# Spreading eight rows of scalars over the partitions: by indicator matmuls, or by DMA

## The chip, the cores and the metric

One core of a Trainium2 chip runs the whole kernel as one program. The metric is the device time in microseconds (us) of one execution. Five engines work side by side: TensorE (PE, matrix products into PSUM), VectorE (DVE), ScalarE (ACT), GpSimd (POOL) and SyncE (SP, which here only issues DMAs). They wait for each other by semaphores. All data is fp32; large products are made of three, from a high and a low part of each operand.

## The reference

```python
x = x + attn(cond(x, side, side, w1, u1, c), Wq, Wk, Wv, Wo, q_scale, k_scale)
x = x + ffn(cond2(x, side, side, w2, u2, c), gate_w, mask_up_w, gate_proj_w, up_proj_w, down_proj_w, inv_map)
```

x is 4 x 256 tokens of 256 channels. cond is a two-sided scan over the tokens, attn a causal attention with 16 heads over 4 key heads, and ffn a feed-forward stage with 8 groups of 176 rows. In ffn each token takes its 8 best of 64 experts. The weights of the chosen experts of one group, added up, give one scalar for each token and group; within a group the experts' shares are a softmax, which weighs a correction that is added to gate and up. Row r of group g then is silu(gate) * up * scalar[g, token], and the down product goes over all 8 x 176 = 1408 rows.

## The kernel before

Channels lie on partitions, tokens along the rows of SBUF. The tokens are worked in two pairs of 512 (PT_). Each engine runs a list of steps, made by `make_plan`: first the scans and the attention of both pairs (32 items), then from about 324 us the feed-forward stage. This stage has 11 tiles of 128 of the 1408 rows (FT = 11) for each pair, 22 tiles in all, numbered f; f = 11 is the first of the second pair. FFN_ORDERS says in which order an engine takes its steps of tile f:

- PE: GA and GB (gate and up of tile f: six products each of 128x512, and one with the expert table EX, two in tile 5 of a pair), GS (line 1289), Y (the down product of tile f-2, six products), and a routing step of the second pair while there are any.
- ACT: GT (tanh, line 792), a routing step, the cast that splits the weights of tile f+3 into high and low part (line 637), GH (the cast of the result to its high part OH, line 800).
- POOL: the low part of the weights of tile f+3 (line 567, three chunks), GL (the low part OL of the result, line 593).
- DVE: GU, three operations: with gate (1078), with up (1082), with the scalars (1087).

The scalars take this way. In step ("route", p, 4) DVE adds the weights of each group into g8a (954) and copies them into STS at columns 0 to 7 and 32 to 39 (956, 957), the rest of which POOL cleared. In ("route", p, 8) PE turns STS (1246) into proj, ACT casts it to SCX (784), and DVE makes the low part in partitions 32 to 39 (980). IND is an indicator: rows g and 32+g are 1 at the columns of group g. It is loaded in two blocks ("ind"), through the three stage buffers that all weights share, and cast by ACT (725). The product GS of a tile of IND with SCX then gives in PSUM (ov) the scalar of each row's group for all 512 tokens. GS waits until the DVE has used the tile before (a_ready), as there is one ov.

SP issues loads in the order of PE's plan; the load into a stage buffer waits for the split of the block that was in it (split_lo, counted by POOL). Weights of tile f+4 therefore load once those of f+1 are split.

Of the kernel before, what the change touches and what calls it, by code (L numbers as in the profile page):

```python
# [6 lines left out]
ALU = mybir.AluOpType  # L7
# [19 lines left out]
NSTAGE, NSLOT, NPS = 3, 6, 4  # L27
# [5 lines left out]
def table_col(g):  # L33
# [24 lines left out]
    "PE": ["GA", "GB", "GS", "Y", "last", "split"],  # L58
# [18 lines left out]
def kv_k(p, half):  # L77
# [17 lines left out]
    "PE": {"R": None, "split": None, "small": None, "ind": None, "K1": None, "V": None, "K3": None, "GA": None, "GB": None,  # L95
           "GS": None, "route": (0, 1, 3, 4, 6, 7, 8)},
    "ACT": {"split": None, "small": None, "ind": None, "K1": None, "V": None, "K2": None, "K3": None, "table": None,
            "wkv": (1, 6, 7), "gate": (0, 1), "route": (0, 2, 3, 5, 6, 7, 8)},
    "DVE": {"K1": None, "K2": None, "table": None, "onehot": None, "wkv": (0, 2, 3, 4, 5, 6, 8), "gate": (0, 1),
            "route": (1, 2, 4, 5, 6, 7, 8)},  # L100
# [14 lines left out]
def make_plan(engine, order, ffn_order):  # L115
# [8 lines left out]
    for i, st in ((2, ("split", "V", 0)), (0, ("R", 6)), (0, ("R", 7)), (0, ("table", 0)), (2, ("table", 1)),  # L124
                  (1, ("onehot",)), (16, ("zeros",)), (24, ("ind", 0)), (32, ("ind", 1)),
                  (11, ("split", "K", 1)), (18, ("split", "V", 1))):
        put(bg, i, st)
# [25 lines left out]
    for f, places in enumerate(([36, 37, 38], [45, 45, 45])):  # L153
        for kind, i in zip(("GA", "GB", "GS"), places):
            if i < END:
                put(bg, i, (kind, f))
                ahead.append((kind, f))
# [61 lines left out]
BLOCKS = [s for s in PLAN if s[0] in ("small", "split", "ind") or s[0] == "R" and s[1] >= 6]  # L219
# [3 lines left out]
BLOCK_COLS = {"R": 4 * FI, "small": 256, "ind": FT * P // 2, "K": 1024, "V": 1024, "Q": 1024, "O": 1024, "F": 768}  # L223
# [84 lines left out]

def program(nc, ins, out):
    ctx = ExitStack()  # L310
    with ctx:
# [31 lines left out]
        IND = sb("IND", [P, FT * P], F32R)  # L343
# [28 lines left out]
        SCX = sb("SCX", [P, B * T], F32R)  # L372
# [22 lines left out]
        STS = sb("STS", [P, TPP, P])  # L395
# [17 lines left out]
        pads_ready decay_ready init_act init_dve zeros_ready key_scale_ready bmask_ready onehot_ready indicator_ready  # L413
# [24 lines left out]
        def wait_proj_free(eng, step):  # L438

            n = PROJ[step]  # L440
            if n == 0:
                return
            q = PROJ_STEPS[n - 1]
            if q[0] in ("K1", "A"):
                eng.wait_ge(s["square_ready"], TOK[q] + 1)
            elif q[0] == "V":
                eng.wait_ge(s["v_ready"], VNO[q] + 1)
            elif q[2] in (0, 3):
                eng.wait_ge(s["rt_act"], RT_ACT[q[2]] + 7 * q[1])
            else:  # L450
                eng.wait_ge(s["rt_vec"], RT_VEC[q[2]] + 7 * q[1])
# [3 lines left out]
        RT_VEC = {1: 1, 2: 2, 4: 3, 5: 4, 6: 5, 7: 6, 8: 7}  # L455
# [84 lines left out]
        def _(pool):  # L540
# [13 lines left out]
            for st in PLANS["POOL"]:  # L554
# [19 lines left out]
                elif st[0] == "zeros":  # L574
                    pool.memset(STS[:], 0.0).then_inc(s["zeros_ready"], 1)
# [22 lines left out]
        def _(act):  # L598
# [13 lines left out]
            for st in PLANS["ACT"]:  # L612
# [109 lines left out]
                elif st[0] == "ind":  # L722
                    w, blk = FT * P // 2, BLOCK_NO[st]
                    act.wait_ge(staged[blk % NSTAGE], 16 * (blk // NSTAGE + 1))
                    nc.scalar.copy(IND[:, w * st[1]:w * st[1] + w], stage[:, blk % NSTAGE, 0:w]).then_inc(s["indicator_ready"], 1)
# [40 lines left out]
                elif st[0] == "route":  # L766
# [16 lines left out]
                    if k == 8:  # L783
                        nc.scalar.copy(SCX[:, tok], proj[:]).then_inc(s["rt_act"], 1)
# [19 lines left out]
        def _(dve):  # L804
# [112 lines left out]
            def route(p, k):  # L917
# [33 lines left out]
                elif k == 4:  # L951
                    dve.wait_ge(s["proj_full"], PROJ[("route", p, 4)] + 1)
                    linked(v.tensor_copy(FL, pj))
                    linked(v.tensor_reduce(g8a[:], FL.rearrange("p a (g j) -> p a g j", g=G), X, ALU.add))
                    dve.wait_ge(s["zeros_ready"], 2)
                    linked(v.tensor_copy(STS[:, :, 0:G], g8a[:]))
                    linked(v.tensor_copy(STS[:, :, 32:32 + G], g8a[:]))
# [20 lines left out]
                elif k == 8:  # L978
                    dve.wait_ge(s["rt_act"], 7 * p + 7)
                    last(v.tensor_tensor(SCX[32:64, tok], proj[32:64, :], SCX[32:64, tok].bitcast(F32), ALU.subtract))  # L980

            for st in PLANS["DVE"]:
# [90 lines left out]
                elif st[0] == "GU":  # L1073
# [9 lines left out]
                    dve.wait_ge(s["scal_full"], f + 1)  # L1083
# [3 lines left out]
                    v.scalar_tensor_tensor(out=PR[:, 4 + f % 2, :], in0=PR[:, 2 + f % 2, :], scalar=0.5, in1=ov[:],  # L1087
# [12 lines left out]
        def _(pe):  # L1100
# [30 lines left out]
            for st in PLAN:  # L1131
# [85 lines left out]
                elif st[0] == "route":  # L1217
# [13 lines left out]
                    elif k == 3:  # L1231
                        pe.wait_ge(s["rt_vec"], 7 * p + RT_VEC[2])
# [7 lines left out]
                    elif k in (6, 7):  # L1240
                        pe.wait_ge(s["rt_vec"], 7 * p + RT_VEC[5])
                        for t in range(TPP):
                            i = tp(proj[:, P * t:P * t + P], ST[:, t, k - 6, :, :, :].rearrange("p g d e -> p (g d e)"), ident)
                    elif k == 8:
                        for t in range(TPP):
                            i = tp(proj[:, P * t:P * t + P], STS[:, t, :], ident)
                    i.then_inc(s["proj_full"], 1)
                elif st[0] in ("GA", "GB"):
# [25 lines left out]
                    pe.wait_ge(s["rt_vec"], 7 * p + 6)  # L1274
# [86 lines left out]
```

## Time and profile before

| | us |
|---|---|
| median of 3 runs (442.9, 447.45, 446.42) | 446.42 |
| profiled execution, its own time | 446.21 |
| its span, first to last instruction | 444.2 |

| engine | busy, us | share |
|---|---|---|
| PE | 380.3 | 86% |
| PE, loading weights | 305.6 | 69% |
| DVE | 336.3 | 76% |
| ACT | 290.4 | 65% |
| POOL | 214.8 | 48% |

Matrix products overlap on PE, so the length of one is more than the time from its start to the next one's. A share is a mean over stages with different limits; what a change in one stage does is read from the rows of that stage. All times of rows are from the start of the span.

### The profile page before, as it was taken

To read this page: it belongs to the slowest core of one execution; us is meant where nothing else is said; L and a number is where in the kernel's file an instruction comes from. 1 tells how busy PE (TensorE), PEld (TensorE's weight loads), DVE (VectorE), ACT (ScalarE), POOL (GpSimd) and SP (SyncE) were. 2 spreads that over 40 slices of the span, in tenths; PEclk is the share of its full clock that TensorE was granted. 3 is DMA by queue.
4 is the path that set the end of the run, shared out by engine and by line. 5 is a ranking of instruction groups with operands and counts; after the bars stand their busy time and mean duration, and the time that the engine had idled before them with its cause. 6 is when DMAs were issued, how large, how long until landed. Compare 5 with 4: busy or idle time off the path is not lost.

```text
span 444.2 us, 6572 instructions
## 1 busy us (share of the span) xinstructions
PE 380.3 (86%) x1974; PEld 305.6 (69%) x1974; DVE 336.3 (76%) x834; ACT 290.4 (65%) x675; POOL 214.8 (48%) x236
## 2 busy tenths in 40 slices
PE   0097866799998869997889798899899999999996
PEld 0086644587877557875758686777678887888884
DVE  6999577999998997577999979866657758553443
ACT  5444868699889768886789995979366334444321
POOL 4671520637553735513159121237138865687632
PEclk9998999999999997999999899999999999999999
DMA  7813410102111110110102200012112321233101
GB/s 201 312 32 106 137 43 0 49 1 97 47 49 48 49 47 0 49 49 0 47 2 82 80 0 2 0 38 71 38 53 90 106 53 56 72 108 94 61 0 47
DMA packets 11073, 26.84 MB, mean 60 GB/s; under 512 B 1312, under 2 KB 3872, under 8 KB 11040
## 3 DMA queue, kind: packets, MB, share of 16 engines
q1 hardware_dynamic: 11040, 26.44, 18.6%
q8 instruction: 16, 0.26, 0.2%
q14 instruction: 17, 0.14, 0.1%
HBM read 25.39 MB, written 1.05 MB: 60 GB/s over the span
## 4 chain that ended last, share of the span: by engine, by line
PE 49%; DVE 30%; ACT 12%; issue 6%; POOL 1%; DMA 1%; POOLq 0%; SPq 0%; DVEq 0%; ACTq 0%
PE acc L1105 4%; PE ov L1198 4%; PE acc L1106 4%; PE acc L1107 4%; PE tr L1127 4%; PE sc L1176 3%; DVE B L845 3%; DVE PR L1037 3%; DVE F L845 3%; ACT PR L600 3%; PE proj L1105 3%; PE proj L1107 2%; PE proj L1106 2%; DVE SS L902 2%; PE tr L1105 2%
## 5 line engine op out<-in xcount | busy, mean ns | idle before, releaser
L567 POOL TENSOR_TENSOR WL<-stage,WH 128x256 fp32r<-128x256 f32 x146 | 119.8, 851 | 112.7 <-ACT WH L637 112.6
L587 POOL TENSOR_TENSOR PR<-PR,RI 128x512 f32<-128x512 f32 x48 | 54.0, 1140 | 89.1 <-DVE RI L1051 89.1
L1105 PE MATMUL proj<-WH,RH 128*128 128x512 f32 x96 | 43.5, 453 | 39.3 <-DVE RL L896 22.9
L600 ACT ACTIVATE PR<-PR,NBI,RQ 128x128 f32<-128x128 f32 (+1 forms) x128 | 68.5, 546 | 1.9 <-DVE NBI L1042 1.7
L1105 PE MATMUL acc<-OH,WH 128*128 128x256 f32 (+1 forms) x172 | 55.4, 322 | 5.2 <-DVE OL L1063 4.4
L1107 PE MATMUL acc<-OH,WL 128*128 128x256 f32 (+1 forms) x172 | 54.0, 314 | 0.0
L1106 PE MATMUL acc<-OL,WH 128*128 128x256 f32 (+1 forms) x172 | 54.0, 314 | 0.0
L1176 PEld LDWEIGHTS sc<-kT,QT 128*128 128x128 f32 x256 | 40.8, 191 | 18.9 <-issue 14.1
L1105 PEld LDWEIGHTS proj<-WH,RH 128*128 128x128 f32 x96 | 19.0, 198 | 47.1 <-issue 42.5
L1176 PE MATMUL sc<-kT,QT 128*128 128x128 f32 (+1 forms) x256 | 47.5, 328 | 2.9 <-DVE MX L1037 2.9
L1198 PE MATMUL ov<-PTS,V 128*128 128x512 f32 x96 | 47.0, 598 | 1.4 <-DVE OL L1063 1.4
L637 ACT CAST WH<-stage 128x768 fp32r<-128x768 f32 (+1 forms) x42 | 39.4, 938 | 2.2 <-DMA stage<-in_wk 2.2
L1078 DVE SCALAR_TENSOR_TENSOR PR<-PR,sc 128x512 f32<-128x512 f32 x22 | 15.1, 685 | 32.2 <-ACT PR L792 32.2
L1107 PE MATMUL proj<-WH,RL 128*128 128x512 f32 x96 | 39.4, 410 | 0.0
L1106 PE MATMUL proj<-WL,RH 128*128 128x512 f32 x96 | 39.1, 408 | 0.0
L1037 DVE CUSTOM_DVE_ANT_0 PR<-sc,const 128x128 f32<-128x128 f32 (+1 forms) x128 | 39.0, 351 | 0.1
L1105 PEld LDWEIGHTS acc<-OH,WH 128*128 128x128 f32 x172 | 33.4, 194 | 7.9 <-issue 5.0
L593 POOL TENSOR_TENSOR OL<-PR,OH 128x512 fp32r<-128x512 f32 x22 | 28.7, 1307 | 12.6 <-ACT OH L800 12.6
L902 DVE TENSOR_REDUCE SS<-SQ 128x4 f32<-128x512 f32 x40 | 27.0, 677 | 10.3 <-ACT SQ L692 10.2
L1106 PEld LDWEIGHTS acc<-OL,WH 128*128 128x128 f32 x172 | 33.5, 195 | 1.7
L1107 PEld LDWEIGHTS acc<-OH,WL 128*128 128x128 f32 x172 | 33.4, 194 | 1.7
L800 ACT CAST OH<-PR 128x512 fp32r<-128x512 f32 x22 | 13.7, 622 | 30.3 <-PE acc L1107 28.4
(167 smaller groups left out, 913.1 us busy)
## 6 DMA issues: line engine op xcount, KB each, us to landing
stage<-in_ffn SPq DMA_DIRECT2D x22, 384.0 KB, 3.1
stage<-in_wq SPq DMA_DIRECT2D x8, 512.0 KB, 3.5
stage<-in_wo SPq DMA_DIRECT2D x8, 512.0 KB, 3.5
PR<-in_tables SPq DMA_DIRECT2D x4, 352.0 KB, 7.1
fT<-in_fT SPq DMA_DIRECT2D x4, 256.0 KB, 4.2
xT<-in_xT SPq DMA_DIRECT2D x4, 256.0 KB, 4.1
stage<-in_wk SPq DMA_DIRECT2D x2, 512.0 KB, 4.6
stage<-in_wv SPq DMA_DIRECT2D x2, 512.0 KB, 3.6
```

The lines of the kernel that those rows point to most:

```text
L567: i = pool.tensor_tensor(lo[:, c:c + 256], src[:, c:c + 256], hi[:, c:c + 256].bitcast(F32), ALU.subtract)
L587: pool.tensor_tensor(pr, pr, RI[:, m % 4, hs[0]:hs[0] + nh].rearrange("p (h o) -> p h o", o=1).broadcast_to([P, nh, 512 // nh]), ALU.mult) ...
L593: pool.tensor_tensor(OL[:, sl], PR[:, 4 + f % 2, :], OH[:, sl].bitcast(F32), ALU.subtract).then_inc(s["a_lo"], 1)
L600: return nc.scalar.activation(o, i, ACT.Exp, **k)
L637: nc.scalar.copy(WH[:, slot, 0:w], src[:, 0:w]).then_inc(s["split_hi"], 1)
L902: v.tensor_reduce(SS[:, n % NST, half_, :], SQ[:, e % 2, :].rearrange("p (h n) -> p h n", h=REP), X, ALU.add).then_inc(s["sumsq_done"], 1)
L1037: i = v.tensor_tensor_reduce(PR[:, u % 6, w * k:w * k + w], sc[u % 2][:, w * k:w * k + w], mask[:, 256 - w:256], 1.0, NEG_BIG, ALU.add, AL ...
L1105: mm(o, lh, rh, start=first, stop=False, skip_group_check=True)
L1106: mm(o, lh, rl, start=False, stop=False, skip_group_check=True)
L1107: return mm(o, ll, rh, start=False, stop=last, skip_group_check=True)
L1176: i = mm(sc[u % 2][:, w * k:w * k + w], QT[:, m % 3, h, :], kT[:, g, T * bb:T * bb + w], start=True, stop=True)
L1198: i = mm(ov[:], V[:, 2 * bb + c, g * D:(g + 1) * D], PTS[:, m % 2, c, :, :].rearrange("p h n -> p (h n)"), start=(c == 0), stop=(c == ti))
```

## The change

The indicator, its loads and casts, the product GS and the low part of the scalars go. DVE adds the groups into SG8, PE turns it into 8 rows, and ACT copies these to SCR, 8 partitions of 1024 tokens, in plain fp32. SP then issues DMAs that read one row of 512 tokens of SCR (2 KB in one partition) and write it into each partition of the tile that belongs to that group. A tile of 128 rows has one or two groups, so one or two DMAs: 18 for a pair, 36 in all. The target is SBC with three buffers (NBC), and the third operation of DVE reads it there, in place of PSUM.

```diff
-NSTAGE, NSLOT, NPS = 3, 6, 4
+NSTAGE, NSLOT, NPS, NBC = 3, 6, 4, 3
-    "PE": ["GA", "GB", "GS", "Y", "last", "split"],
+    "PE": ["GA", "GB", "Y", "last", "split"],
...
+def group_rows(m):
+
+    first, last = P * m // FI, (P * m + P - 1) // FI
+    return [(g, max(g * FI - P * m, 0), min((g + 1) * FI - P * m, P)) for g in range(first, last + 1)]
...
+            def spread_scalars(f):
+                p, m = divmod(f, FT)
+                sp.wait_ge(s["rt_act"], 7 * p + 7)
+                if f >= NBC:
+                    sp.wait_ge(s["a_ready"], f - NBC + 1)
+                for g, lo, hi in group_rows(m):
+                    sp.dma_start(SBC[lo:hi, f % NBC, :], SCR[g:g + 1, p * PT_:(p + 1) * PT_].rearrange("g (o n) -> g o n", o=1).broadcast_to([1, hi - lo, PT_])).then_inc(spread_in[f % NBC], 16)
+
             for n in range(6, len(BLOCKS)):
+                if BLOCKS[n][0:2] == ("split", "F") and BLOCKS[n][2] >= 4:
+                    spread_scalars(BLOCKS[n][2] - 4)
                 load(n)
+            for f in range(FT * NPAIR - 4, FT * NPAIR):
+                spread_scalars(f)
...
-                        nc.scalar.copy(SCX[:, tok], proj[:]).then_inc(s["rt_act"], 1)
+                        nc.scalar.copy(SCR[:, tok], proj[0:G, :]).then_inc(s["rt_act"], 1)
...
-                    linked(v.tensor_reduce(g8a[:], FL.rearrange("p a (g j) -> p a g j", g=G), X, ALU.add))
-                    dve.wait_ge(s["zeros_ready"], 2)
-                    linked(v.tensor_copy(STS[:, :, 0:G], g8a[:]))
-                    linked(v.tensor_copy(STS[:, :, 32:32 + G], g8a[:]))
+                    linked(v.tensor_reduce(SG8[:], FL.rearrange("p a (g j) -> p a g j", g=G), X, ALU.add))
+                    dve.wait_ge(s["zeros_ready"], 1)
...
-                elif k == 8:
-                    dve.wait_ge(s["rt_act"], 7 * p + 7)
-                    last(v.tensor_tensor(SCX[32:64, tok], proj[32:64, :], SCX[32:64, tok].bitcast(F32), ALU.subtract))
...
-                    dve.wait_ge(s["scal_full"], f + 1)
+                    dve.wait_ge(spread_in[f % NBC], 16 * spread_count(f))
...
-                    v.scalar_tensor_tensor(out=PR[:, 4 + f % 2, :], in0=PR[:, 2 + f % 2, :], scalar=0.5, in1=ov[:],
+                    v.scalar_tensor_tensor(out=PR[:, 4 + f % 2, :], in0=PR[:, 2 + f % 2, :], scalar=0.5, in1=SBC[:, f % NBC, :],
...
-                            i = tp(proj[:, P * t:P * t + P], STS[:, t, :], ident)
+                            i = tp(proj[0:G, P * t:P * t + P], SG8[:, t, :], ident)
...
-                elif st[0] == "GS":
-                    f = st[1]
-                    p, m = divmod(f, FT)
-                    if f:
-                        pe.wait_ge(s["a_ready"], f)
-                    else:
-                        pe.wait_ge(s["o_lo"], 32)
-                        pe.wait_ge(s["indicator_ready"], 2)
-                    pe.wait_ge(s["rt_vec"], 7 * p + 7)
-                    mm(ov[:], IND[:, P * m:P * m + P], SCX[:, p * PT_:(p + 1) * PT_], start=True, stop=True).then_inc(s["scal_full"], 1)
```

On SP before, the loads of the 22 tiles of weights (in_ffn) follow the last loads of the output weights and of the indicator, and behind them stand only the stores of the result:

```order
L494 DMA stage<-in_wo 128x1024 x2
L494 DMA stage<-in_ind 128x704
L494 DMA stage<-in_ffn 128x768 x22
L535 DMA out<-xT 128x512 x4
L311 UNCONDITIONAL_BRANCH
```

On SP now, at the same place, with the waits in brackets (rt_act counts ACT's routing copies, a_ready the tiles that DVE has finished):

```order
L502 DMA stage<-in_wo 128x1024 [waits split_lo] x3
L502 DMA stage<-in_ffn 128x768 [waits split_lo] x4
L543 DMA SBC<-SCR 128x1x512 [waits rt_act]
L502 DMA stage<-in_ffn 128x768 [waits split_lo]
L543 DMA SBC<-SCR 48x1x512 [waits rt_act]
L543 DMA SBC<-SCR 80x1x512
L502 DMA stage<-in_ffn 128x768 [waits split_lo]
L543 DMA SBC<-SCR 96x1x512 [waits rt_act]
L543 DMA SBC<-SCR 32x1x512
L502 DMA stage<-in_ffn 128x768 [waits split_lo]
L543 DMA SBC<-SCR 128x1x512 [waits a_ready,rt_act]
```

The first four loads stay together; from then on the spread of tile f stands ahead of the load of tile f+4, up to f = 17, and the spreads of the last four tiles follow the last load. From tile 3 on a spread also waits until DVE has finished tile f-3.

On PE before, between the last product of "up" and the down product of an earlier tile, in the feed-forward stage:

```order
L1278 MATMUL tr<-SX,EX 128x512
L1289 MATMUL ov<-SCX,IND 128x512
L1105 MATMUL acc<-OH,WH 128x512
L1106 MATMUL acc<-OL,WH 128x512
L1107 MATMUL acc<-OH,WL 128x512
```

On PE now:

```order
L1288 MATMUL tr<-SX,EX 128x512
L1115 MATMUL acc<-OH,WH 128x512
L1116 MATMUL acc<-OL,WH 128x512
L1117 MATMUL acc<-OH,WL 128x512
L1115 MATMUL acc<-OH,WH 128x512
```

The product L1289 is gone and nothing else has moved.

## Rows read from the trace of the kernel before

**Rows 1.** The page: busy us of each engine, share of the span, instructions.
```profile
PE 380.3 (86%) x1974; PEld 305.6 (69%) x1974; DVE 336.3 (76%) x834; ACT 290.4 (65%) x675; POOL 214.8 (48%) x236
```
**Rows 2.** Stretches: length, busy us (instructions) of each engine, granted clock, DMA share, GB/s.
```profile
332.00:362.00 30.00, 30.00 (x137) 24.45 (x135) 20.43 (x41) 15.09 (x24) 21.99 (x24) 1.00 0.27 79
386.00:432.00 46.00, 46.00 (x205) 38.09 (x204) 21.42 (x32) 17.56 (x28) 31.91 (x37) 1.00 0.21 64
```
**Rows 3.** PE's timeline, two tiles: start us, us, engine, line, names, shape.
```profile
425.99 0.39 PE L1289 MATMUL ov<-SCX,IND 128*128 128x512 f32 x1
...
430.75 0.39 PE L1289 MATMUL ov<-SCX,IND 128*128 128x512 f32 x1
```
**Rows 4.** What writes ov: durations in ns, min/median/max, first and last start.
```profile
L1289 PE MATMUL ov<-SCX,IND x22: 389/389/389, 331.8 to 435.5; 128*128 128x512 f32 x22
```
**Rows 5.** Timelines of DVE and PE at the first pair's group sums.
```profile
314.35 0.18 DVE L956 COPY STS<-g8a 128x32 f32<-128x32 f32 x1
...
314.79 0.29 DVE L958 TENSOR_SCALAR RT<-RT 128x256 f32<-128x256 f32 x1
...
317.20 0.35 PE L1105 MATMUL acc<-OH,WH 128*128 128x256 f32 x1 [0.95 <-DVE OL L1063]
```
**Rows 6.** Timeline of ACT: the scalars of the first and of the second pair.
```profile
327.53 0.59 ACT L784 CAST SCX<-proj 128x512 fp32r<-128x512 f32 x1 [1.07 <-PE proj L1246]
...
384.45 0.59 ACT L784 CAST SCX<-proj 128x512 fp32r<-128x512 f32 x1 [2.90 <-PE proj L1246]
```
**Rows 7.** The casts of the indicator.
```profile
L725 ACT CAST IND<-stage x2: 797/798/800, 241.0 to 303.4; 128x704 fp32r<-128x704 f32 x2
```
**Rows 8.** The four stores of the result, 256 KB each, from issue to landing.
```profile
DMA to landing us min/median/max: 2.0/2.8/3.8
```
**Rows 9.** DMA from 440 to 444.2, two stores: GB/s in 40 slices, the queue.
```profile
GB/s 0 0 0 0 0 0 0 0 0 0 0 0 0 0 0 0 0 0 195 429 371 371 371 351 332 332 429 371 371 410 390 234 39 0 0 0 0 0 0 0
...
q1 hardware_dynamic: 288, 0.52, 33.4%
```
**Rows 10.** DMA from 395 to 398.5, one load of 384 KB.
```profile
q1 hardware_dynamic: 144, 0.39, 38.2%
```
**Rows 11.** Timeline of DVE, ACT and POOL at the first tiles of the second pair.
```profile
388.44 0.69 DVE L1087 SCALAR_TENSOR_TENSOR PR<-PR,ov 128x512 f32<-128x512 f32 x1
...
389.30 0.62 ACT L800 CAST OH<-PR 128x512 fp32r<-128x512 f32 x1 [1.79 <-PE acc L1107]
...
390.83 0.60 ACT L792 ACTIVATE PR<-sc 128x512 f32<-128x512 f32 x1 [0.91 <-PE sc L1278]
...
391.33 0.83 ACT L637 CAST WH<-stage 128x768 fp32r<-128x768 f32 x1
391.33 1.31 POOL L593 TENSOR_TENSOR OL<-PR,OH 128x512 fp32r<-128x512 f32 x1
...
392.58 2.17 POOL L567 TENSOR_TENSOR WL<-stage,WH 128x256 fp32r<-128x256 f32 x3
```
**Rows 12.** Timeline of DVE and ACT at the last tile.
```profile
436.49 0.69 DVE L1087 SCALAR_TENSOR_TENSOR PR<-PR,ov 128x512 f32<-128x512 f32 x1
...
437.35 0.62 ACT L800 CAST OH<-PR 128x512 fp32r<-128x512 f32 x1 [2.63 <-PE acc L1107]
...
440.38 1.38 DVE L1096 TENSOR_TENSOR xT<-xT,acc 128x512 f32<-128x512 f32 x2 [3.20 <-PE acc L1107]
```
**Rows 13.** A stretch as in rows 2, and PE's timeline in it.
```profile
164.00:170.00 6.00, 3.65 (x14) 3.02 (x15) 5.79 (x22) 3.34 (x8) 3.17 (x4) 0.64 0.20 79
...
166.34 1.94 PE L1127 MATMUL tr<-const,RT 128*128 128x128 f32 x8 [3.08 <-DVE PTS L1057]
```
**Rows 14.** Timeline of DVE and POOL at the first tiles of the first pair.
```profile
333.18 0.69 DVE L1087 SCALAR_TENSOR_TENSOR PR<-PR,ov 128x512 f32<-128x512 f32 x1
...
333.64 3.13 POOL L567 TENSOR_TENSOR WL<-stage,WH 128x256 fp32r<-128x256 f32 x3 [2.51 <-ACT WH L637]
333.78 1.68 DVE L990 SCALAR_TENSOR_TENSOR TH<-TH,fT 128x1024 f32<-128x1024 f32 x1
```

More of the change, by code:

```diff
@@ L94 @@
 RELEVANT = {
-    "PE": {"R": None, "split": None, "small": None, "ind": None, "K1": None, "V": None, "K3": None, "GA": None, "GB": None,
-           "GS": None, "route": (0, 1, 3, 4, 6, 7, 8)},
-    "ACT": {"split": None, "small": None, "ind": None, "K1": None, "V": None, "K2": None, "K3": None, "table": None,
+    "PE": {"R": None, "split": None, "small": None, "K1": None, "V": None, "K3": None, "GA": None, "GB": None,
+           "route": (0, 1, 3, 4, 6, 7, 8)},
+    "ACT": {"split": None, "small": None, "K1": None, "V": None, "K2": None, "K3": None, "table": None,
             "wkv": (1, 6, 7), "gate": (0, 1), "route": (0, 2, 3, 5, 6, 7, 8)},
     "DVE": {"K1": None, "K2": None, "table": None, "onehot": None, "wkv": (0, 2, 3, 4, 5, 6, 8), "gate": (0, 1),
-            "route": (1, 2, 4, 5, 6, 7, 8)},
+            "route": (1, 2, 4, 5, 6, 7)},
     "POOL": {"split": None, "small": None, "zeros": None},
@@ L124, in make_plan @@
     for i, st in ((2, ("split", "V", 0)), (0, ("R", 6)), (0, ("R", 7)), (0, ("table", 0)), (2, ("table", 1)),
-                  (1, ("onehot",)), (16, ("zeros",)), (24, ("ind", 0)), (32, ("ind", 1)),
+                  (1, ("onehot",)), (16, ("zeros",)),
                   (11, ("split", "K", 1)), (18, ("split", "V", 1))):
@@ L153, in make_plan @@
     for f, places in enumerate(([36, 37, 38], [45, 45, 45])):
-        for kind, i in zip(("GA", "GB", "GS"), places):
+        for kind, i in zip(("GA", "GB"), places):
             if i < END:
@@ L217 @@
 PLAN = PLANS["PE"]
-BLOCKS = [s for s in PLAN if s[0] in ("small", "split", "ind") or s[0] == "R" and s[1] >= 6]
+BLOCKS = [s for s in PLAN if s[0] in ("small", "split") or s[0] == "R" and s[1] >= 6]
 BLOCK_NO = {s: n for n, s in enumerate(BLOCKS)}
@@ L222 @@
 SPLIT_NO = {s: n for n, s in enumerate(SPLITS)}
-BLOCK_COLS = {"R": 4 * FI, "small": 256, "ind": FT * P // 2, "K": 1024, "V": 1024, "Q": 1024, "O": 1024, "F": 768}
+BLOCK_COLS = {"R": 4 * FI, "small": 256, "K": 1024, "V": 1024, "Q": 1024, "O": 1024, "F": 768}
 PROJ_SPLITS = [s for s in SPLITS if s[0] == "split" and s[1] in "KVQ"]
@@ L306, with spread_count @@
         unit_tr[units_before(_m) + _j] = TR[("D", _m, _j)]
+def group_rows(m):
+    first, last = P * m // FI, (P * m + P - 1) // FI
+    return [(g, max(g * FI - P * m, 0), min((g + 1) * FI - P * m, P)) for g in range(first, last + 1)]
+def spread_count(f):
+    return sum(len(group_rows(k % FT)) for k in range(f % NBC, f + 1, NBC))
 def program(nc, ins, out):
@@ L342, in program @@
         GWL = sb("GWL", [P, CH, 128], F32R)
-        IND = sb("IND", [P, FT * P], F32R)
         RH = sb("RH", [P, NPAIR, CH, PT_], F32R)
@@ L371, in program @@
         SX = sb("SX", [P, 2, B * T], F32R)
-        SCX = sb("SCX", [P, B * T], F32R)
+        SCR = sb("SCR", [G, B * T])
+        SBC = sb("SBC", [P, NBC, PT_])
         bmask = V[:, :, :].rearrange("p t n -> p (t n)").rearrange("p (c g d e) -> p c g d e", c=CH, g=G, d=16)
@@ L394, in program @@
         ST = sb("ST", [P, TPP, 2, 4, 4, GS])
-        STS = sb("STS", [P, TPP, P])
+        SG8 = sb("SG8", [P, TPP, G])
         def gate1(b):
@@ L412, in program @@
         names = """consts_in vecs_in cond_in side_in0 side_in1 side_in2 side_in3 x_in0 x_in1 x_in2 x_in3 table_in0 table_in1 table_in2 table_in3 table_in4 table_in5 mup_in imap_in stores_done
-        pads_ready decay_ready init_act init_dve zeros_ready key_scale_ready bmask_ready onehot_ready indicator_ready
+        pads_ready decay_ready init_act init_dve zeros_ready key_scale_ready bmask_ready onehot_ready
         split_hi split_lo ffn_used
@@ L417, in program @@
         scores_full max_ready bias_ready exp_done rinv_ready p_ready pt_act pt_dve ov_full o_hi o_lo wo_done x1_ready
-        gate_full up_full scal_full first_rows tanh_done gate_used up_used a_ready a_hi a_lo y_full result_ready
+        gate_full up_full first_rows tanh_done gate_used up_used a_ready a_hi a_lo y_full result_ready
         den_log rt_act rt_vec dve_link act_link pool_link""".split()
@@ L421, in program @@
         staged = [sem(f"staged{k}") for k in range(NSTAGE)]
+        spread_in = [sem(f"spread_in{k}") for k in range(NBC)]
         block = ctx.enter_context(nc.Block())
@@ L447, in wait_proj_free @@
                 eng.wait_ge(s["v_ready"], VNO[q] + 1)
-            elif q[2] in (0, 3):
+            elif q[2] in (0, 3, 8):
                 eng.wait_ge(s["rt_act"], RT_ACT[q[2]] + 7 * q[1])
             else:
-                eng.wait_ge(s["rt_vec"], RT_VEC[q[2]] + 7 * q[1])
+                eng.wait_ge(s["rt_vec"], RT_VEC[q[2]] + 6 * q[1])
         RT_ACT = {0: 1, 2: 2, 3: 3, 5: 4, 6: 5, 7: 6, 8: 7}
-        RT_VEC = {1: 1, 2: 2, 4: 3, 5: 4, 6: 5, 7: 6, 8: 7}
+        RT_VEC = {1: 1, 2: 2, 4: 3, 5: 4, 6: 5, 7: 6}
         def wait_turned(eng, t):
@@ L574, in _ @@
                 elif st[0] == "zeros":
-                    pool.memset(STS[:], 0.0).then_inc(s["zeros_ready"], 1)
                     pool.wait_ge(s["wkv_dve"], last_call(1, B - 1))
@@ L721, in _ @@
                     i.then_inc(s["table_hi"], 1)
[L722 to L725, printed above, removed]
                 elif st[0] == "B":
@@ L775, in _ @@
                     if k == 2:
-                        act.wait_ge(s["rt_vec"], 7 * p + RT_VEC[1])
+                        act.wait_ge(s["rt_vec"], 6 * p + RT_VEC[1])
                         exp(LG, LG).then_inc(s["rt_act"], 1)
                     if k == 5:
-                        act.wait_ge(s["rt_vec"], 7 * p + RT_VEC[4])
+                        act.wait_ge(s["rt_vec"], 6 * p + RT_VEC[4])
                         exp(MR, MR).then_inc(s["rt_act"], 1)
@@ L1231, in _ @@
                     elif k == 3:
-                        pe.wait_ge(s["rt_vec"], 7 * p + RT_VEC[2])
+                        pe.wait_ge(s["rt_vec"], 6 * p + RT_VEC[2])
                         for t in range(TPP):
@@ L1240, in _ @@
                     elif k in (6, 7):
-                        pe.wait_ge(s["rt_vec"], 7 * p + RT_VEC[5])
+                        pe.wait_ge(s["rt_vec"], 6 * p + RT_VEC[5])
                         for t in range(TPP):
@@ L1273, in _ @@
                         three(bank[:], w[0], w[1], RH[:, p, ch, :], RL[:, p, ch, :], ch == 0, False)
-                    pe.wait_ge(s["rt_vec"], 7 * p + 6)
+                    pe.wait_ge(s["rt_vec"], 6 * p + 6)
                     if f == 0:
@@ L1329 @@
                                  np.where(np.arange(P) % 32 // GS == 1, -1.0, 0.0).astype(f32)[:, None]], axis=1)
-    ind = np.zeros((P, FT * P), f32)
-    for g in range(G):
-        ind[g, g * FI:(g + 1) * FI] = 1.0
-        ind[32 + g, g * FI:(g + 1) * FI] = 1.0
-    a["ind"] = ind
     a["imap"] = np.ascontiguousarray(np.broadcast_to(i["L0_ffn_inv_map"].reshape(1, E), (E, E))).astype(np.int32)
```

4 lines of the change are left out of this document (removed).

## The prediction

> **What bounds the kernel now.** The page comes first: TensorE (PE) is busy for 86% of the span, more than any other engine [rows 1]. The table of stretches then shows where that holds. In the feed-forward stage PE has no idle time at all: 30.00 of 30.00 us from 332 to 362 and 46.00 of 46.00 from 386 to 432, at full granted clock, while VectorE (DVE), ScalarE (ACT) and GpSimd (POOL) are idle for a quarter of it or more [rows 2]. PE's timeline gives the beat: the indicator product of one tile starts at 425.99 and that of the next at 430.75, so a tile takes 4.76 us, 21 products 0.227 us apart (one is issued every 0.227, though each lasts 389 ns, since they overlap) [rows 3]. So before the change the stage runs at PE's beat and everything else has slack.
>
> **What is removed.** 22 indicator products, one per tile, of 389 ns each [rows 4], worth 0.227 us each at PE's beat: 22 x 0.227 = 5.0 us of PE. The tile drops from 4.76 to 4.53 us if PE still sets the beat. In each pair's routing, DVE loses two copies into STS (314.35 to 314.79, 0.44 us, ahead of the OL subtraction for which PE sits idle for 0.95 us in the first pair) [rows 5], and after the last transposes the subtraction of SCX, that stands behind ACT's cast of SCX [rows 6]. ACT loses two casts of IND of 0.80 us [rows 7], POOL a memset, SP two loads; none of them stands in front of an idle PE, so I count them as nothing, and they cannot cost anything.
>
> **What is added.** 22 spreads. Each reads one row (512 fp32, 2 KB) of SCR and writes it into up to 128 partitions: 128 packets of 2 KB, 256 KB in all, sent as one or two DMAs. The bytes written are those of one store of the output. But the source is special: all 128 packets read the same partition (a split tile reads two, neighbours). In a store, sixteen queues each read their own eight partitions. No row of this trace shows many queues reading one partition, so I bound it.
>
> From below, a spread lands like a store of 256 KB: 2.0 to 3.8 us, 2.8 in the median [rows 8]. From above, the row behaves like what one queue alone moves, packet after packet: in the window that holds the last two stores the queues worked 33.4% of 16 x 4.2 us = 22.4 us for 256 packets of data, 0.088 us each, so 128 packets one at a time take 11.2 us. The fullest slices of that window show 429 GB/s, 26.8 per queue: at that rate 256 KB through a single reader takes 9.8 us [rows 9]. Between ends so far apart (2.8 and 11.2) I take 9.8: the reading side is one partition, and what the trace shows that one partition, or the eight of a queue, ever gives at once is one queue's flow. With sixteen queues asking there is always a next packet, hence the rate of the fullest slice and not that of the mean.
>
> The Trainium skill prices just this (SBUF — State Buffer, Door 1: The DMA port swizzle): partitions share 16 ports, partitions 0 to 3 lie on one, and 27.6 GB/s was measured through it, 27.2 as its limit. By that page a spread is an estimated 262144 B / 27.2 GB/s = 9.6 us, and the total below would be 564; no run here shows it yet.
>
> **Why it is then on the path.** 9.8 us is more than twice the 4.53 us of a tile. NBC = 3 buffers keep up to three spreads in the queue, so the fixed latency hides, but the flow does not: DVE's last product of tile f waits for spread f, and OH, OL and the down product follow it. The order also puts load F(f+4) behind spread f on the same SP queue. A load of 384 KB occupies the queues for 38.2% of 16 x 3.5 = 21.4 us, 1.34 each [rows 10]. Queues that end their share of the spread early can start on it, so between 0 and 1.34 us is added per load; I take 0.7. A wait that could add more: spread f+1 is issued only after load F(f+4), which waits until tile f+1's weights are split on POOL, and that split now stands behind tile f-3's OL. From landing f-3 it takes 0.69 (DVE) + 0.62 (OH) + 0.60 (tanh) + 0.83 (cast) + about 3.5 (OL and the three chunks) = 6.2 us [rows 11], while spreads f-2 to f are queued, over 20 us of work. So it never starves. PE's 20 products (4.5 us) lie inside each 10 us.
>
> **The sum.**
> - First spread issued when ACT has copied the scalars: 327.53 + 0.59 = 328.1 [rows 6], less 0.4 for the STS copies: 327.7.
> - It lands after the fixed part of a store (2.0 least landing, less the 0.7 that the packets take: 22.4/16/2 per store [rows 8, 9]) 1.3, and 9.8: 338.8.
> - 21 more spreads: 21 x 9.8 = 205.8. 18 loads (F4 to F21) between them: 18 x 0.7 = 12.6. Last landing at 557.2. The second pair's first spread waits for its own scalars, ready some 3 us after spread 9 lands, when spread 10 is still moving: no gap.
> - Tail: from the last scaling on DVE at 436.49 to the end of the span at 444.2 it is now 7.7 us, OH, OL, six products, the addition and the store [rows 12]. That stays: 564.9.
> - PE idles for half of each tile. From 164 to 170, where it had stood idle for 3.08 us, the granted clock is 0.64 of full, a mixture of both levels [rows 13]. At 1.2 GHz the last six products take 1.3 us more: 566.2. Elsewhere PE at 1.2 GHz (9 us per tile) still fits into 10.
> - The profiled execution took 446.2 us beside a span of 444.2: 2.0 around it. 568.2. It lies at the median of the runs (446.42), so nothing is corrected.
>
> The 5.0 us taken from PE are worth nothing here, since PE no longer sets the beat. Upper end: 11.2 per spread (22 x 1.4 = 30.8) and 1.34 per load (+11.5): 611. Lower end: loads free (-12.6) and no loss of clock (-1.3): 554.
>
> **Rivals.** *Hidden* (the other side). If a spread lands like a store, in 2.8 us, it is there at 330.5, ahead of the first scaling at 333.18 [rows 14]; for tile 11 the scalars are ready at 385.04 [rows 6] and it lands at 387.8 against 388.44 [rows 11]. At 3.8 us it is 0.4 late there; OH of that tile waits for PE until 389.30 anyway, and PE needs the tile two tiles later. Then PE keeps the beat: 21 x 0.227 = 4.8, 0.1 at the last tile (DVE ends at 437.18, and OH waits until 437.35 for PE [rows 12]), 0.6 for the STS copies in two pairs: 440.7 us. It decides as long as spread and load together fit in 4.53 us. A second thing touches this rival: the scaling now reads both inputs from SBUF. Where DVE does that today (L990), three POOL chunks take 3.13 us instead of 2.17 [rows 11, 14]. At most 0.69 us per tile is 3 x 0.74 + 1.30 + 0.69 = 4.2 us of POOL, still under 4.53: nothing.
>
> The Trainium skill also has a rule that speaks for this rival (SBUF — State Buffer, Summary: rules for kernel authors): between SBUF and SBUF reckon with 436 GB/s. That would be an estimated 0.6 us of moving, and the change would be worth its 5 us. I hold it to be meant for transfers over all partitions, as the stores here are (up to 429 in a slice).
>
> *Two packets at a time* from a partition: 4.9 us, 5.6 with a load, still over 4.53. 327.7 + 1.3 + 22 x 4.9 + 12.6 + 7.7 + 2.0 = 459 us.
>
> *Slower than one queue*: if one partition gives half of a queue's rate, 19.6 us per spread, 568 + 22 x 9.8 = 784 us; for 640 it takes 13.1. What speaks for it is only that a queue's flow in the trace comes from eight partitions in turn.
>
> **Chances.** One queue's rate (554 to 611): 0.66. Slower than that: 0.09. Two or more packets at a time, but not hidden: 0.09. Hidden: 0.16. The prediction is 568 us. For 8 in 10 the range must take in the two-packet case and the near part of the slow one: 455 to 640; the likeliest case alone has 554 to 611. About 1% is what a measurement of this kernel tells from no change. The hidden case gains 1.3%, of which a small loss leaves less than 1%: it gives 0.10 to faster and 0.05 to same; the rest of it and of the two-packet case that may come out within 1% adds 0.01. Slower has 0.84.
>
> **What would show it.** Right: the landing time of SBC<-SCR at 10 us and more (more where several are queued), DVE's scaling line with some 100 us of idle time ended by DMA, the DMA share over 0.9 through the feed-forward stage at only about 30 to 40 GB/s, PE at half, tiles some 10.5 us apart for the first 18 and 9.8 for the last four, the stage before 327 unmoved. Wrong: landings of about 3 us and a PE without idle time at 4.53 us per tile (hidden), a beat near 5.6 (two packets), tiles over 12 us apart (slower than a queue), or a beat that is long while the queues stand empty: then it is the waits of SP and not the reading.

## The result and the profile after

The changed kernel takes 550.75 us (median of 4 runs, 550.19 to 553.22), the kernel before 445.08 us (median of 4, 442.9 to 447.45). The ratio is 1.238, interval 1.230 to 1.247: slower by almost a quarter. The profiled execution took 550.44 us with a span of 548.7.

In what follows a spread is the one or two DMAs that bring a tile its scalars. It lands when its semaphore shows that all of it has arrived. The scaling is DVE's third operation of a tile, which reads the spread, and the beat is the distance from the start of one tile's scaling to that of the next.

Stretches of the changed kernel, columns as in [rows 2]:

```profile
332.00:362.00 30.00, 19.28 (x74) 14.64 (x73) 8.47 (x11) 7.18 (x12) 11.62 (x14) 0.77 0.92 67
386.00:432.00 46.00, 30.73 (x122) 23.76 (x122) 17.91 (x29) 11.39 (x19) 17.24 (x21) 0.83 0.91 63
...
521.50:539.50 18.00, 5.86 (x12) 3.66 (x12) 4.14 (x6) 2.23 (x4) 2.54 (x2) 0.67 0.88 46
```

PE, without a gap before, is busy for two thirds of the time in the first two stretches and for a third in the last, and part of that at the lower level of its clock (mean granted clock 0.67 to 0.83 of full). No engine is near its limit. What is full is the second column from the right: the DMA queues are busy for 88 to 92% of the time (27 and 21% before) and move no more than 46 to 67 GB/s (79 and 64 before).

What the queues did from 430 to 480, and the three sizes of DMA with the longest part in it (40 slices of GB/s; KB each, median us from issue to landing):

```profile
GB/s 26 26 116 282 31 26 26 26 26 61 223 107 28 26 28 28 26 80 216 103 28 28 28 26 26 102 212 79 26 26 28 26 29 132 196 62 26 29 26 26
...
q1 hardware_dynamic: 1510, 3.32, 92.1%
...
stage<-in_ffn SPq DMA_DIRECT2D x5, 384.0 KB, 14.1
SBC<-SCR SPq DMA_DIRECT2D x2, 256.0 KB, 15.7
```

The first row points at the cause. While only a spread moves, all sixteen queues together make 26 to 28 GB/s in most slices; in [rows 9] sixteen queues made 429 in the fullest slices, 26.8 each, so this is what one of them made there. In between stand the loads of weights, whose fullest slices show 196 to 282 GB/s.

Who waited, us in total, times, longest:

```profile
ACT OH L815 <- DVE PR L1097: 154.7, 22, 8.7
DVE PR L1097 <- DMA SBC<-SCR: 131.6, 22, 7.2
POOL OL L612 <- ACT OH L815: 124.6, 22, 8.5
PEld acc L1115 <- POOL OL L612: 49.8, 12, 7.6
```

The scaling on DVE waits for the spread in each of the 22 tiles, for 131.6 us in all; ACT's cast waits for the scaling, POOL for the cast and PE for POOL. The starts of the scaling give the beat:

```profile
338.75 0.69 DVE L1097 SCALAR_TENSOR_TENSOR PR<-PR,SBC 128x512 f32<-128x512 f32 x1 [7.17 <-DMA SBC<-SCR]
348.55 0.69 DVE L1097 SCALAR_TENSOR_TENSOR PR<-PR,SBC 128x512 f32<-128x512 f32 x1 [6.45 <-DMA SBC<-SCR]
358.41 0.69 DVE L1097 SCALAR_TENSOR_TENSOR PR<-PR,SBC 128x512 f32<-128x512 f32 x1 [6.51 <-DMA SBC<-SCR]
...
378.01 0.69 DVE L1097 SCALAR_TENSOR_TENSOR PR<-PR,SBC 128x512 f32<-128x512 f32 x1 [6.50 <-DMA SBC<-SCR]
387.20 0.69 DVE L1097 SCALAR_TENSOR_TENSOR PR<-PR,SBC 128x512 f32<-128x512 f32 x1 [4.11 <-DMA SBC<-SCR]
...
521.58 0.69 DVE L1097 SCALAR_TENSOR_TENSOR PR<-PR,SBC 128x512 f32<-128x512 f32 x1 [6.44 <-DMA SBC<-SCR]
531.35 0.69 DVE L1097 SCALAR_TENSOR_TENSOR PR<-PR,SBC 128x512 f32<-128x512 f32 x1 [6.42 <-DMA SBC<-SCR]
539.52 0.69 DVE L1097 SCALAR_TENSOR_TENSOR PR<-PR,SBC 128x512 f32<-128x512 f32 x1 [4.82 <-DMA SBC<-SCR]
```

9.8 us per tile at the start, with loads between the spreads, and 9.77 near the end (521.58 to 531.35), with none. 256 KB in 9.8 us is 26.7 GB/s. Before, the beat was 4.76 us [rows 3].

### The profile page after: what moved, and what is told of

The parts are those of the page before. It is cut to its first block, busy times and chain, and to the rows that moved or that the text cites. A ratio compares the mean times of both kernels' runs of the same rounds, so it can differ in the third digit from the quotient of the medians.

```text
span 548.7 us, 6550 instructions
## 1 busy us (share of the span) xinstructions
PE 396.1 (72%) x1952; PEld 309.8 (56%) x1952; DVE 333.1 (61%) x828; ACT 287.2 (52%) x673; POOL 213.5 (39%) x235
## 4 chain that ended last, share of the span: by engine, by line
DVE 23%; PE 22%; SPq 17%; DMA 14%; ACT 13%; issue 7%; POOL 2%; POOLq 0%; ACTq 0%; DVEq 0%
DMA SBC<-SCR 14%; SPq L543 12%; SPq L502 5%; PE ov L1208 3%; ACT PR L619 3%; PE tr L1137 3%; DVE B L860 2%; PE sc L1186 2%; PE proj L1115 2%; DVE PR L1047 2%; DVE F L860 2%; PE acc L1115 2%; PE proj L1117 2%; PE proj L1116 2%; PE acc L1116 2%
## 5 line engine op out<-in xcount | busy, mean ns | idle before, releaser
L587 POOL TENSOR_TENSOR WL<-stage,WH 128x256 fp32r<-128x256 f32 x146 | 117.4, 834 | 105.6 <-ACT WH L656 105.5
L1115 PE MATMUL acc<-OH,WH 128*128 128x256 f32 (+1 forms) x172 | 60.6, 352 | 60.0 <-POOL OL L612 44.4
L1097 DVE SCALAR_TENSOR_TENSOR PR<-PR,SBC 128x512 f32<-128x512 f32 x22 | 15.2, 692 | 131.6 <-DMA SBC<-SCR 131.6
L1115 PEld LDWEIGHTS acc<-OH,WH 128*128 128x128 f32 x172 | 34.7, 202 | 68.1 <-POOL OL L612 49.8
L1116 PE MATMUL acc<-OL,WH 128*128 128x256 f32 (+1 forms) x172 | 57.7, 335 | 0.0
L1117 PE MATMUL acc<-OH,WL 128*128 128x256 f32 (+1 forms) x172 | 57.7, 335 | 0.0
L1117 PEld LDWEIGHTS acc<-OH,WL 128*128 128x128 f32 x172 | 35.2, 205 | 2.8
L1116 PEld LDWEIGHTS acc<-OL,WH 128*128 128x128 f32 x172 | 35.2, 205 | 1.7
L917 DVE TENSOR_REDUCE SS<-SQ 128x4 f32<-128x512 f32 x40 | 27.0, 677 | 11.1 <-ACT SQ L711 10.9
## 6 DMA issues: line engine op xcount, KB each, us to landing
stage<-in_ffn SPq DMA_DIRECT2D x22, 384.0 KB, 14.1
```

What stands on the lines that cost most here:

```text
L587: i = pool.tensor_tensor(lo[:, c:c + 256], src[:, c:c + 256], hi[:, c:c + 256].bitcast(F32), ALU.subtract)
L1115: mm(o, lh, rh, start=first, stop=False, skip_group_check=True)
L1116: mm(o, lh, rl, start=False, stop=False, skip_group_check=True)
L1117: return mm(o, ll, rh, start=False, stop=last, skip_group_check=True)
```

## The experiments

**Another source.** The spread reads row for row from an SCR widened to 128 partitions. PE and ACT fill it from a scratch tensor, so this kernel leaves out the scalars of the groups; the DMAs differ in their source alone:

```diff
-sp.dma_start(SBC[lo:hi, f % NBC, :], SCR[g:g + 1, p * PT_:(p + 1) * PT_].rearrange("g (o n) -> g o n", o=1).broadcast_to([1, hi - lo, PT_])).then_inc(spread_in[f % NBC], 16)
+sp.dma_start(SBC[lo:hi, f % NBC, :], SCR[lo:hi, p * PT_:(p + 1) * PT_]).then_inc(spread_in[f % NBC], 16)
```

> The changed kernel with one thing other: each spread reads row for row from 128 partitions of a wider SCR, no longer one partition for all. Same number of DMAs, same bytes, same order, same waits (the values of the scalars are wrong: this leaves out the choice of the group's row). Theory A (one partition gives about 26.8 GB/s to all readers together): spreads land in 2 to 4 us, DVE's scaling never waits for DMA, PE keeps a beat of 4.53 us per tile, total 440 to 443 us. Rival B (36 more DMAs and their waits on SP hold up the loads): stays at about 550 us, long issue times on SP. Rival C (DMA between SBUF and SBUF is slow by itself): stays at about 550 us.

Measured: 440.69 us against 444.29 of the kernel before, run beside it, ratio 0.994 (0.991 to 0.997). The same 36 DMAs of the same bytes in the same order now land so (us, least, median, longest):

```profile
DMA to landing us min/median/max: 1.9/3.2/5.0
```

For the changed kernel this row reads:

```profile
DMA to landing us min/median/max: 12.1/14.9/22.6
```

(These are from the issue, at which the spread ahead is still moving; so it is more than 9.8.) DVE never waited for a spread, and PE was busy for 46.00 of 46.00 us from 386 to 432. So neither the number of DMAs, nor their order on SP, nor DMA between SBUF and SBUF as such makes the change slow (rivals B and C). The source does: one partition, read by all.

**Half the row.** The spread copies 256 of the 512 tokens, 1 KB packets, and DVE reads the half twice. The kernel leaves out the scalars of the other half.

```diff
-SCR[g:g + 1, p * PT_:(p + 1) * PT_].rearrange("g (o n) -> g o n", o=1).broadcast_to([1, hi - lo, PT_])
+SCR[g:g + 1, p * PT_:p * PT_ + PT_ // 2].rearrange("g (o n) -> g o n", o=1).broadcast_to([1, hi - lo, PT_ // 2])
```

> The changed kernel with spreads of 256 of the 512 tokens (1 KB packets, same 36 DMAs, same single source partition); DVE reads the half twice, so the second half of each pair's tokens gets wrong scalars. Theory A: 4.9 us per spread, against a PE beat of 4.53: 326.6 + 1.3 + 22 x 4.9 + 7.7 to 9.2 + 1.7 = 445 to 447 us, the beat set by DMA by a hair. Rival B (count and order of DMAs): about 550 us still. Rival D (a fixed price per packet at one partition, whatever its size): 9.8 us per spread still, about 550 us.

Measured: 450.21 us, ratio 1.016 (1.011 to 1.021). In the second pair the scaling mostly starts every 5.0 us and still waits for DMA:

```profile
396.23 0.69 DVE L1097 SCALAR_TENSOR_TENSOR PR<-PR,SBC 128x512 f32<-128x512 f32 x1 [1.60 <-DMA SBC<-SCR]
...
401.24 0.69 DVE L1097 SCALAR_TENSOR_TENSOR PR<-PR,SBC 128x512 f32<-128x512 f32 x1 [1.65 <-DMA SBC<-SCR]
```

Half the bytes, half the beat: it is a flow and no price per packet (rival D). It came out 3 us above the forecast: in the middle of the first pair PE, which has the second pair's routing to do there, is slower than 5 us per tile, and the spreads have to start anew for the second pair (the first scaling there waits 3.89 us). This fits the prediction's condition, that a spread costs time once it takes longer than PE's 4.53 us: at 5.0 us it costs 1.6% of the kernel's time, at 9.8 us 24%. No run lies closer to 4.53.

**Partition or port?** After its last store the kernel before issues more DMAs, each waited for, with nothing else running (the waits between them are left out here):

```diff
+sp.dma_start(dst[:, 0:512], src[0:1, 0:512].rearrange("g (o n) -> g o n", o=1).broadcast_to([1, P, 512])).then_inc(s["probe"], 16)   # L538
+sp.dma_start(dst[:, 0:512], src[:, 0:512]).then_inc(s["probe"], 16)             # L540
+sp.dma_start(dst[:, 0:512], ins["wk"][0:1, 0:512].broadcast_to([P, 512])).then_inc(s["probe"], 16)   # L542
+sp.dma_start(dst[0:16:4, :], src[0:4, :]).then_inc(s["probe"], 16)              # L544, 4 rows of 12 KB
+sp.dma_start(dst[0:16:4, :], src[0:16:4, :]).then_inc(s["probe"], 16)           # L546
+sp.dma_start(dst[0:4, :], src[0:16:4, :]).then_inc(s["probe"], 16)              # L548
+sp.dma_start(dst[:, 0:512], src[0:1, 0:512].rearrange("g (o n) -> g o n", o=1).broadcast_to([1, P, 512])).then_inc(s["probe"], 16)   # L550
+sp.dma_start(dst[:, 512:1024], src[4:5, 0:512].rearrange("g (o n) -> g o n", o=1).broadcast_to([1, P, 512])).then_inc(s["probe2"], 16)   # L551, not waiting for L550
```

> The kernel before, and after its last store eight DMAs one after the other, each waited for (the last two together), nothing else running. Expected landings by theory A as it stands (the limit is a port shared by several partitions): one partition to 128, 256 KB: 1.3 + 9.8 = 11 us; 128 to 128 partitions, 256 KB: 2.0; one HBM row to 128: 2 to 3; partitions 0 to 3 to partitions 0, 4, 8, 12, 48 KB: 1.3 + 1.8 = 3.1; partitions 0, 4, 8, 12 to the same: 1.3 + 0.45 = 1.8; partitions 0, 4, 8, 12 to 0 to 3: 3.1 if writing is limited like reading; two spreads at once from partitions 0 and 4: the second lands at 11 to 12 us after its issue if they lie on two ports and the queues overlap, at 21 if not. Rival E (the limit is the single partition, not a port): partitions 0 to 3 land in 1.8 us like 0, 4, 8, 12.

SP's timeline. Each DMA is issued when the one ahead has landed, so the distance of two starts is the landing time of the first (that of L538 starts at 438.0):

```profile
449.26 0.54 SPq L540 DMA_DIRECT2D PR<-stage  x1
451.66 0.35 SPq L542 DMA_DIRECT2D PR<-in_wk  x1
454.73 0.74 SPq L544 DMA_DIRECT2D PR<-stage  x1
458.36 0.63 SPq L546 DMA_DIRECT2D PR<-stage  x1
460.66 0.58 SPq L548 DMA_DIRECT2D PR<-stage  x1
464.05 0.53 SPq L550 DMA_DIRECT2D PR<-stage  x1
465.02 0.53 SPq L551 DMA_DIRECT2D PR<-stage  x1
```

| DMA | expected | landed after, us |
|---|---|---|
| one partition to 128, 256 KB | 11 | 11.3 |
| 128 to 128 partitions, 256 KB | 2.0 | 2.4 |
| one HBM row to 128, 256 KB | 2 to 3 | 3.1 |
| partitions 0 to 3 to 0, 4, 8, 12, 48 KB | 3.1 | 3.6 |
| partitions 0, 4, 8, 12 to the same | 1.8 | 2.3 |
| partitions 0, 4, 8, 12 to 0 to 3 | 3.1 | 3.4 |

Each of these DMAs ran once, in one execution. Four neighbouring partitions take 1.3 us longer to read than four partitions that lie four apart. 48 KB at 26.8 GB/s are 1.8 us and at four times that 0.5, a difference of 1.4. Nor did the neighbours' packets go one after the other: each DMA is four packets of 12 KB (and four small ones), and in the 3.63 us of the one (L544) they took 11.5% of sixteen queues' time, 1.7 us each, about as long as all four together need at that rate; in the other (L546) it was 7.3% of 2.30 us, 0.7 us each. So the limit is not the single partition (rival E), but something that partitions 0 to 3 share and 0, 4, 8, 12 do not. Writing to 0 to 3 also took 1.1 us longer, but there the packets took only 0.5 us each, so what holds it up is not seen in them. The two spreads at once took until 17.8 us after the second was issued, 18.8 for both: two in a row at 9.8 are 19.6 and the fixed part. So two sources that don't share the limit overlap little. That each queue works through the first spread before it comes to the second would explain it; no run tests this. The trace of the changed kernel has the same little gain: where a tile takes its rows from group 3 and group 4, and so reads partition 3 and partition 4, its scaling follows after 9.2 us in the first pair (378.01 to 387.20 above) and 8.6 in the second, not 9.8.

**By way of HBM.** Each pair's eight rows are stored to HBM first (16 KB) and the spreads read them there, the whole result being computed:

```diff
+if m == 0:
+    sp.dma_start(bounce[:, p * PT_:(p + 1) * PT_], SCR[:, p * PT_:(p + 1) * PT_]).then_inc(s["bounced"], 16)
+    sp.wait_ge(s["bounced"], 16 * p + 16)
...
-    sp.dma_start(SBC[lo:hi, f % NBC, :], SCR[g:g + 1, ...]...
+    sp.dma_start(SBC[lo:hi, f % NBC, :], bounce[g:g + 1, p * PT_:(p + 1) * PT_].broadcast_to([hi - lo, PT_])).then_inc(spread_in[f % NBC], 16)
```

> The changed kernel, but each pair's 8 rows are first stored to HBM (16 KB, SP waits for the landing), and the spreads read them there; result complete. Theory A: the single partition is no longer read, so spreads land in about 3 us; the store adds some 2 us ahead of tiles 0 and 11, where 2 to 3 us are spare; 441 to 444 us, below the kernel before. Rival C: HBM reads are as quick as those of loads, same result. If 128 reads of one HBM row are as serial as those of one partition, about 550 us.

Measured: 442.34 us against 444.29, ratio 0.996 (0.992 to 0.999); once more, beside dram_psum below, 443.05 against 444.8, 0.997 (0.994 to 0.999).

> via_dram once more, on the same chip as dram_psum, for the comparison of the two: 0.996 of the kernel before, as measured.

128 reads of one row of HBM are as quick as a spread from 128 partitions: landings of 1.9 to 5.8 us, 3.4 in the median (1.9, 5.0 and 3.2 in wide_source). Only the first spread of each pair is late, by 0.76 and 1.89 us, and the second lateness reaches no idle PE (46.00 of 46.00 us busy from 386 to 432).

**Two buffers.** NBC = 2 in the changed kernel.

> The changed kernel with NBC = 2: a spread is issued once DVE has finished the tile two before, not three. Theory A (flow of the one reader): at that moment one spread of 9.8 us is still moving, the next is issued 1 us after the landing, so nothing changes, 549 to 552 us. Rival F (the waits of SP for a free buffer set the beat, three buffers being just too few): one less buffer adds about the fixed part of a landing, 1.3 to 2 us per tile, 30 us and more in all, 580 us or above.

Measured, in one execution: 551.12 us, the beat unchanged (first scaling at 339.3, last at 540.2, in place of 338.7 and 539.5). The waits for a free buffer don't set the beat (rival F falls).

**One SBUF input in place of two.** wide_source and via_dram gained less than the 5.5 us that the prediction gave the hidden case. In wide_source the scaling, which now reads PR and SBC, both in SBUF, took 0.69 us at times and much more at others. Its durations in ns, least, median, longest:

```profile
L1098 DVE SCALAR_TENSOR_TENSOR PR<-PR,SBC x22: 692/1080/1611, 332.9 to 432.8; 128x512 f32<-128x512 f32 x22
```

and the longest one beside POOL, in their timelines:

```profile
341.56 1.61 DVE L1098 SCALAR_TENSOR_TENSOR PR<-PR,SBC 128x512 f32<-128x512 f32 x1
```

```profile
341.33 1.29 POOL L613 TENSOR_TENSOR OL<-PR,OH 128x512 fp32r<-128x512 f32 x1
343.29 2.13 POOL L588 TENSOR_TENSOR WL<-stage,WH 128x256 fp32r<-128x256 f32 x3 [0.68 <-ACT WH L657]
```

POOL's operation ends at 342.62 and the scaling, started early in it, at 343.17, 0.55 us later: it has waited for POOL. The Trainium skill says so (SBUF — State Buffer, Who interferes with whom): a DVE operation with two SBUF inputs and a GpSimd one that reads SBUF exclude each other, whichever comes second waits until the first is done. The trace agrees: 1.61 us here, and 0.69 us in every tile before, with ov in PSUM. To test what it costs, the second operation writes to the PSUM bank that the indicator product has left free (in tile 0 it first waits until the attention has done with that bank):

```diff
-v.tensor_tensor(PR[:, 2 + f % 2, :], PR[:, 2 + f % 2, :], tr[f % 2][:], ALU.mult).then_inc(s["up_used"], 1)
+v.tensor_tensor(ov[:], PR[:, 2 + f % 2, :], tr[f % 2][:], ALU.mult).then_inc(s["up_used"], 1)
...
-v.scalar_tensor_tensor(out=PR[:, 4 + f % 2, :], in0=PR[:, 2 + f % 2, :], scalar=0.5, in1=SBC[:, f % NBC, :],
+v.scalar_tensor_tensor(out=PR[:, 4 + f % 2, :], in0=ov[:], scalar=0.5, in1=SBC[:, f % NBC, :],
```

> via_dram with one thing other: DVE's second operation of a tile (with up) writes its result to the PSUM bank ov, which no indicator product uses any more, and the third reads it there beside SBC. So the scaling has one input in SBUF, not two. Theory S (the scaling with two SBUF inputs holds up POOL and is held up by it: 0.69 to 1.61 us in wide_source, three POOL chunks up to 3.6 us, and PE waits 1.4 to 1.6 us for it in the first pair): the scaling takes 0.69 us in every tile, POOL's chunks 2.2 us beside it, and the total is 1 to 1.6 us below via_dram. Rival (the loss in the first pair has another source, the store ahead of the spreads): no difference to via_dram.

Measured: 441.98 us against 444.8, ratio 0.994 (0.992 to 0.997). The scaling:

```profile
L1105 DVE SCALAR_TENSOR_TENSOR PR<-ov,SBC x22: 690/692/693, 329.9 to 428.6; 128x512 f32<-128x512 f32 x22
```

Every one takes 0.69 us. What this is worth is read from PE, by the last product of "up" in tiles 2 and 3; first via_dram2:

```profile
337.28 0.39 PE L1293 MATMUL tr<-SX,EX 128*128 128x512 f32 x1
...
344.56 0.39 PE L1293 MATMUL tr<-SX,EX 128*128 128x512 f32 x1
```

then dram_psum:

```profile
334.58 0.39 PE L1296 MATMUL tr<-SX,EX 128*128 128x512 f32 x1
...
340.49 0.39 PE L1296 MATMUL tr<-SX,EX 128*128 128x512 f32 x1
```

7.28 us has become 5.91, and before the change it was 6.12, with one indicator product (0.227 us) more. From tile 0 to tile 21 the same product is at a distance of 99.17 us in dram_psum, 100.82 in via_dram2 and 103.71 before: 1.65 us less than via_dram2, 1.37 of them from tile 2 to 3. In the total it is 1.1 us below via_dram2. The intervals of the two ratios (0.992 to 0.997 and 0.994 to 0.999) overlap, but run against run dram_psum is the quicker one in 115 of 144 pairs. So the mechanism is shown, and a worth of about 1 us is likely, but its size is not pinned down. (Only one execution of each was traced, and that of dram_psum was the quickest of its twelve, 438.37 us; so only distances within the stage are set side by side.)

## Why the prediction was right

**That it gets slower, and where.** Right. The source of the spreads sets the beat, with PE idle for a third of the time and more, at a reduced clock, and the 5.0 us taken from it without effect. Of the signs it named, 30 to 40 GB/s was too low (63 to 67 in the two long stretches): a spread and a load in a beat of 10.5 us make 62, by its own sizes.

**Price of a spread.** 9.8 us was taken, from the fullest slices of a store [rows 9]; measured 9.8 from scaling to scaling, and 11.3 alone with its fixed part, for which 11.1 had been reckoned. That the fullest slice, and not the mean, gives the limit was a choice, and it held. The first scaling was forecast at 338.8 and came at 338.75, which is luck: the spread was issued at 326.63, 1.1 us ahead of the 327.7 reckoned, and no spread landed in less than 12.1 us, where 11.1 had been reckoned. The prediction also took the single partition, or the eight of a queue, as what is limited; the runs show that partitions 0 to 3 share the limit. For the price of a spread this makes no difference, as a tile reads one row or two. The Trainium skill's 9.6 us would have done as well: by its port limit (SBUF — State Buffer, Door 1: The DMA port swizzle) the total was 564. Here the runs back it in more than the price: by that section partitions 0 to 3 lie on one port, and these four read together took 3.6 us where 0, 4, 8 and 12 took 2.3.

**Price of a load between the spreads.** Wrong: 0.7 us for each of 18, 12.6 in all; measured 0. The beat is 9.8 us with loads (348.55 to 358.41) and 9.77 without (521.58 to 531.35). As the spreads are held by their source and not by the queues, a load finds room: its fullest slices show 196 to 282 GB/s in the middle of it. It was in the range, as the lower end (554), and it makes up most of the distance from 568 to 550.

**21 spreads of 9.8.** 205.8 forecast, 200.8 measured (338.75 to 539.52). The distance from one tile to the next is less than 9.8 in four places: 7.7 at the last tile of the first pair and 8.2 at that of the second (531.35 to 539.52), where no spread stood behind it for most or all of its time, and 9.2 and 8.6 where a tile reads groups 3 and 4. This had no term in the sum: 5.0 us. That a spread behind competes for the source and so delays the one ahead is a reading of these distances, not tested.

**Tail and clock.** 7.7 + 1.3 = 9.0 forecast, 9.2 measured (539.52 to 548.7). The six products of the last tile start 0.43 us apart, against 0.227 [rows 3]:

```profile
542.85 0.63 PE L1116 MATMUL acc<-OL,WH 128*128 128x512 f32 x1
543.28 0.63 PE L1117 MATMUL acc<-OH,WL 128*128 128x512 f32 x1
543.70 0.63 PE L1115 MATMUL acc<-OH,WH 128*128 128x512 f32 x1
```

Together: 568.2 - 12.6 (loads) - 5.0 (distances) + 0.2 (tail) - 0.3 (around the span, 1.7 in place of 2.0) = 550.5, and the profiled execution took 550.44.

**SP's waits.** Right that they never starve the queues, though not by the reckoning alone: two_buffers shows it. The prediction had three spreads queued, over 20 us of work, but a spread landed 14.9 us after its issue in the median, one and a half beats, and 14.0 with two buffers. What was not foreseen is where SP spends its time, see below.

**The hidden rival** was not the case here, but wide_source is this rival made real, and it measures its sum: forecast 1.2% faster, measured 0.6% (0.3 to 0.9%), 3.6 us in place of 5.5. The steps that failed: two SBUF inputs were priced by what they cost POOL, and so at nothing; they cost DVE too, up to 0.9 us in a tile, and the output's low part comes later for it. And the copies into STS (0.6 us in two pairs) brought nothing that shows. From tile 11 to the last, where PE alone sets the beat, the 10 x 0.227 = 2.3 us are there in full (48.05 us from 388.44 to 436.49 before, 45.79 in wide_source). In the first pair, where DVE and POOL also carry the routing, 1.1 us came of 2.5 (55.26 before, 54.14 in wide_source, tile 0 to 11). PE's own distances, by the last product of "up" from tile 0 to 11, say the same, 55.65 and 54.54, and in dram_psum, without the shared reading, it is 53.38: 2.3 us of the 2.5 are there. So the shared reading took about 1.2 us of the 1.4 that were missing; where the last 0.2 went is open.

## What to carry to other kernels

Reckon a DMA by what its source and its target have in common, not by bytes over the total rate: sixteen queues that read one partition of SBUF shared 26 to 28 GB/s here, so a row of 2 KB to 128 partitions cost 9.8 us, and reading the neighbours 0 to 3 together was slowed as if they were one. Before a broadcast from one partition is put into a loop, compare this with the loop's beat; if it is above, store the few rows to HBM and broadcast from there (3.1 us alone; the kernel is then 0.4% faster than before, not 24% slower). And when a product is replaced by data in SBUF, look at what the reading operation does to GpSimd: a free PSUM bank for the intermediate keeps the two apart.

## What was unexpected

- **The issuing engine is held up inside the instruction.** The duration of the DMA instructions on SP's queue, in ns (least, median, longest), in the changed kernel; a store took 332 to 432 before:

```profile
L543 SPq DMA_DIRECT2D SBC<-SCR x36: 515/2368/9104, 326.6 to 517.7; - x36
```

  SP sits in the issue for up to 9.1 us. Its waits for semaphores then look short, so a table of waits alone hides that it is held up. Loads behind it are held as well (14.1 us to land, 3.1 before), here without harm: in the feed-forward stage no engine's wait ends with a load.
- **Loads ride free on a stream that is limited at its source.** 384 KB with each spread changed the beat by less than 0.1 us, with queues that count as 92% busy. The busy share of queues doesn't say that they are used up; GB/s beside it does.
- **Partitions 0, 4, 8 and 12 don't share the limit, neighbours do**: 3.6 us to read 48 KB from 0 to 3 against 2.3, and 3.4 to write it there, each measured once.
